# Projection stage of a window attention and ConvNeXt kernel: stores in halves on SyncE, first image quantized earlier

## The reference

```python
# layer 0: attention in windows of 7 x 7, every linear layer fake-quantized to int8
xw = x.reshape(B, C, r1, WS, r2, WS).transpose(0, 2, 4, 3, 5, 1).reshape(B * r1 * r2, n, C)
qkv = quant_linear(xw, Wqkv, bqkv)
...
out = jnp.einsum('bhmn,bhnc->bhmc', attn, v)
out = quant_linear(out, Wout, bout)          # fq(out) @ fq(Wout).T + bout: the stage that is changed
out = out.reshape(B, r1, r2, WS, WS, C).transpose(0, 5, 1, 3, 2, 4).reshape(B, C, H, W)
# layer 1: depthwise 7 x 7 convolution, layer norm, MLP with gelu and response norm, residual
y = jax.lax.conv_general_dilated(x, dw_w, (1, 1), [(3, 3), (3, 3)], feature_group_count=C, ...)
...
return residual + y
```

## Time and profile before

| | us |
|---|---|
| median of 3 runs | 5082.19 (5073.92 to 5095.0) |
| profiled execution | 5095.38 |
| its span | 5093.7 |
| projection stage, first operation to the next stage's first load | 2479.5 to 3005.1 |
| busy in the whole span: PE, DVE, ACT, POOL | 4027.8, 3922.3, 3246.1, 1504.5 |
| mean granted clock of TensorE, share of full speed | 0.90 |
| ScalarE waiting for `rd` and `yd` stores in the stage | 79.6 and 52.7 |

### The profile page before, as it was taken

One profiled execution on the slowest core, in us unless ns is written; L12 is line 12 of the kernel. 1 busy time (PEld: TensorE's weight loads), 2 busy tenths in 40 slices (PEclk: granted clock), 3 DMA queues, 4 the chain that ended last, 5 costly groups with the idle time before them and its releaser, 6 DMA issues. The chain is left out here.

```text
span 5093.7 us, 116728 instructions
## 1 busy us (share of the span) xinstructions
PE 4027.8 (79%) x40394; PEld 2551.1 (50%) x40394; DVE 3922.3 (77%) x7112; ACT 3246.1 (64%) x5602; POOL 1504.5 (30%) x1844
## 2 busy tenths in 40 slices
PE   1687777676688988888456669996689999999999
PEld 1233554454577776777444434443345455554544
DVE  7797999999999999999645520001799999999985
ACT  0675777775698988989355644443556666666663
POOL 0201111111666666666422200001232222222210
PEclk9997777876799999999777779998799999999999
DMA  7773666665333333333277778886122222222212
GB/s 316 203 204 107 160 160 166 159 163 143 79 96 94 91 94 91 94 91 94 74 256 254 279 243 290 278 278 200 63 66 90 87 90 76 76 90 87 90 55 68
DMA packets 227952, 725.18 MB, mean 142 GB/s; under 512 B 30346, under 2 KB 128138, under 8 KB 206794
## 3 DMA queue, kind: packets, MB, share of 16 engines
q1 hardware_dynamic: 203402, 589.58, 39.6%
q0 software_dynamic: 24128, 130.26, 7.1%
HBM read 428.25 MB, written 291.50 MB: 141 GB/s over the span
## 5 line engine op out<-in xcount | busy, mean ns | idle before, releaser
L852 POOL TENSOR_TENSOR exp_lo<-exp,exp_hi 128x294 f16<-128x294 f32 x1024 | 773.1, 782 | 374.8 <-ACT exp_hi L923 374.8
L1613 PE MATMUL out_psum<-gelu_hi,w_parts 128*128 128x448 f16 x2016 | 605.0, 355 | 58.9 <-DVE w_parts L1789 31.5
L1649 ACT ACTIVATE gelu_pair<-h_psum,b_rows,w_unscale 128x448 f32<-128x448 f32 x448 | 324.5, 728 | 412.5 <-PE h_psum L1565 224.7
L1685 DVE BATCH_NORM_STATS2 ln_stats<-z_img 128x6 f32<-128x192 f32 x448 | 126.0, 344 | 566.7 <-DMA z_img<-zd 565.9
L1349 PE MATMUL conv_psum<-c_in,toeplitz 128*128 128x448 f16 (+1 forms) x2304 | 470.4, 366 | 68.9 <-DMA dwb<-in_L_conv_dw_b_dram 68.9
L948 DVE SCALAR_TENSOR_TENSOR logit_int<-attn_int,scalars,bias_products 128x588 f16<-128x588 int8 x512 | 488.2, 954 | 38.6 <-ACT attn_int L929 27.0
L1565 PE MATMUL h_psum<-ln_parts_T,w_hi 128*128 128x448 f16 x2016 | 494.3, 354 | 18.1 <-DVE w_in L1748 16.2
L929 ACT ACTIVATE attn_int<-p_psum,scalars 128x588 int8<-128x588 f32 x512 | 389.4, 761 | 174.7 <-PE p_psum L455 163.7
L1613 PE MATMUL out_psum<-gelu_lo,w_parts 128*128 128x448 f16 x1344 | 475.5, 354 | 0.0
L610 PE MATMUL range_psum<-q_diag,k_diag 128*128 128x196 bf16 x1536 | 275.2, 316 | 227.8 <-DVE p_min L692 225.0
L894 PE MATMUL o_psum<-a_v,exp_hi 128*128 128x34 f16 x6144 | 382.8, 179 | 78.4 <-DVE a_o L975 66.3
(11 more groups left out here) (313 smaller groups left out, 9901.8 us busy)
## 6 DMA issues: line engine op xcount, KB each, us to landing
k_diag<-kd SPq DMA_DIRECT2D x128, 384.0 KB, 5.0
toeplitz<-gd SPq DMA_DIRECT2D x48, 1024.0 KB, 17.2
yd<-y_out POOLq DMA_DIRECT2D x16, 2880.0 KB, 28.1
c_in<-yd SPq DMA_DIRECT2D x24, 1920.0 KB, 9.4
zd<-c_out POOLq DMA_DIRECT2D x24, 1792.0 KB, 13.8
z_img<-zd SPq DMA_DIRECT2D x16, 2688.0 KB, 9.4
x_chunk<-in_x_dram SPq DMA_DIRECT2D x12, 3136.0 KB, 10.4
x_img<-in_x_dram SPq DMA_DIRECT2D x16, 2352.0 KB, 15.9
```

The costliest lines, as they stand in the source:

```text
L852: last = nc.gpsimd.tensor_tensor(el[r][:, :, 2 * a, 0:N], src[:, :, a], eh[r][:, :, 2 * a, 0:N], ALU.subtract)
L1613: last = nc.tensor.matmul(po[:, t, 0:TCH], w, hx[:, f, cols], start=f == 0 and x == 0, stop=f == NF - 1 and x == len(steps) - 1)
L1649: nc.scalar.activation(h[y // 2 % 3][:, y % 2], ph[:, y % 3, 0:TCH], ACT.Gelu, scale=k1[:], bias=b1[:, f:f + 1]).then_inc(hd, 1)
```

## The change

Three things change, all in `phase_project`.

- *Stores.* y is computed in two halves of its channels. `NY` becomes 16, eight steps (`NH`) to a half, four row pairs of 96 channels to a step; the last step of a half has one row pair. The residual is stored in two parts, its first four blocks of 448 pixels (`RTOP`) and the other three. SyncE starts these four stores of an image, each with its own semaphore, and ScalarE waits per half.
- *SyncE's order.* Six units are loaded ahead, then per image: load, first halves of y and r, load, second halves.
- *Start.* GpSimd quantizes units 0 and 1 right after clearing `o_in`, and units 2 and 3 right after the all-reduce. VectorE places four of the first image's eight bands before it waits for the all-reduce.

Moved unchanged and not shown: the bodies of `quantize` and `place`.

```diff
...
-        sty = [s.sem(f"y_stored{k}") for k in range(2)]
-        strr = [s.sem(f"r_stored{k}") for k in range(2)]
+        sty = [[s.sem(f"y_stored{k}_{h}") for h in range(2)] for k in range(2)]
+        strr = [[s.sem(f"r_stored{k}_{p}") for p in ("top", "rest")] for k in range(2)]
...
-        NY = (QP + 1) // 2
+        NQ = 4
+        NH = -(-QP // NQ)
+        NY = 2 * NH
+        CH = C // 2
+        RTOP = 4
...
-            def image(i, first):
-                for k in range(2):
-                    for hf in range(2):
-                        u = 4 * i + 2 * k + hf
-                        if not (first and k == 0):
-                            sp.wait_ge(oqd, u - 1)
-                        for h in range(2):
-                            sp.dma_start(oi[hf][64 * h:64 * h + N], s.od[bass.ds(u, 1)].rearrange("u h n j w f -> (u h) n j w f")[h]).then_inc(ld[hf], 16)
-            peeled(sp, IMG // 2, image)
+            def load(u, hf, first):
+                if not first:
+                    sp.wait_ge(oqd, u - 1)
+                for h in range(2):
+                    sp.dma_start(oi[hf][64 * h:64 * h + N], s.od[bass.ds(u, 1)].rearrange("u h n j w f -> (u h) n j w f")[h]).then_inc(ld[hf], 16)
+
+            def store_y(m, k, h):
+                half = slice(h * NCB // 2, (h + 1) * NCB // 2)
+                sp.dma_start(s.yd[half, :, bass.ds(m, 1)].rearrange("b p i c x q -> p (b i) (c x q)"),
+                             y[k][:, h * CH:(h + 1) * CH].rearrange("p (b c) x q -> p b (c x q)", c=CB)).then_inc(sty[k][h], 16)
+
+            def store_r(m, k, part, lo, hi):
+                dst = s.rd[bass.ds(m, 1)].rearrange("i (t p) n -> (i p) t n", t=2)
+                sp.dma_start(dst[:, :, lo:hi], r[k][:, :, lo:hi]).then_inc(strr[k][part], 16)
+
+            def image(i, loads):
+                for k in range(2):
+                    m = 2 * i + k
+                    if loads(k):
+                        load(2 * m + 6, 0, False)
+                    sp.wait_ge(ye, NY * m + NH)
+                    store_y(m, k, 0)
+                    sp.wait_ge(re, 2 * NTC * m + 2 * RTOP)
+                    store_r(m, k, 0, 0, RTOP * TCH)
+                    if loads(k):
+                        load(2 * m + 7, 1, False)
+                    sp.wait_ge(ye, NY * (m + 1))
+                    store_y(m, k, 1)
+                    sp.wait_ge(re, 2 * NTC * (m + 1))
+                    store_r(m, k, 1, RTOP * TCH, TOK)
+
+            for u in range(6):
+                load(u, u % 2, u < 2)
+            with sp.Fori(0, IMG // 2 - 2) as i:
+                image(i, lambda k: True)
+            image(IMG // 2 - 2, lambda k: k == 0)
+            image(IMG // 2 - 1, lambda k: False)
+            for k in range(2):
+                for part in range(2):
+                    sp.wait_ge(sty[k][part], 16 * IMG // 2)
+                    sp.wait_ge(strr[k][part], 16 * IMG // 2)
...
             for k in range(2):
                 link(nc.gpsimd.memset(oi[k][:], 0.0))
...
+            for u in range(2):
+                quantize(u, u, True)
+            pool.wait_ge(oqd, 2)
             pool.wait_ge(otz, 6)
             for k in range(2):
                 link(nc.gpsimd.memset(ot[k][0][CK:CK + NPART, 1:HW + 1, PITCH - HW:PITCH], 1.0))
             pool.wait_ge(ch, LMAX)
             nc.gpsimd.partition_all_reduce(ma[:], mp[:], P, RMAX).then_inc(ar, 1)
+            pool.wait_ge(ar, 1)
+            for u in range(2, 4):
+                quantize(u, u % 2, False)
             pool.wait_ge(ch, LCH)
             for x in range(2):
                 for t in range(2):
                     nc.gpsimd.dma_start(s.gd[x, t * CK:(t + 1) * CK, :], lines[x][:, t, :]).then_inc(lst, 16)
...
-                    pool.wait_ge(ye, NY * (m + 1))
-                    pool.wait_ge(re, 2 * NTC * (m + 1))
-                    pool.dma_start(s.yd[:, :, bass.ds(m, 1)].rearrange("b p i c x q -> p (b i) (c x q)"),
-                                   y[k][:].rearrange("p (b c) x q -> p b (c x q)", c=CB)).then_inc(sty[k], 16)
-                    pool.dma_start(s.rd[bass.ds(m, 1)].rearrange("i (t p) n -> (i p) t n", t=2), r[k][:]).then_inc(strr[k], 16)
-
-            for u in range(4):
-                quantize(u, u % 2, u < 2)
             images(pool, image)
-            for k in range(2):
-                pool.wait_ge(sty[k], 16 * IMG // 2)
-                pool.wait_ge(strr[k], 16 * IMG // 2)
             pool.wait_ge(lst, 64)

...
                     for x in range(NY):
                         if not (first and k == 0 and x < 2):
                             pe.wait_ge(ye, NY * m + x - 1)
-                        for qq in range(2 * x, min(2 * x + 2, QP)):
+                        h, q0 = x // NH, x % NH * NQ
+                        for qq in range(q0, min(q0 + NQ, QP)):
                             for t in range(2):
                                 rows = ot[k][t][:, ROWS - 2 * qq - 2:ROWS - 2 * qq, :].rearrange("p r x -> p (r x)")
-                                last = nc.tensor.matmul(py[:, (x + k * NY) % 2, qq % 2 * C:(qq % 2 + 1) * C], rows, s.woT[t][:],
+                                last = nc.tensor.matmul(py[:, x % 2, (qq - q0) * CH:(qq - q0 + 1) * CH], rows, s.woT[t][:, h * CH:(h + 1) * CH],
                                                         start=t == 0, stop=t == 1)
                         last.then_inc(ym, 1)
                         if x < 2 * NTC:
...
                     for x in range(NY):
                         act.wait_ge(ym, NY * m + x + 1)
-                        if not first and x == 0:
-                            act.wait_ge(sty[k], 16 * i)
-                        nq = min(2, QP - 2 * x)
-                        nc.scalar.activation(y[k][:, :, 0, 2 * x:2 * x + nq],
-                                             py[:, (x + k * NY) % 2, 0:nq * C].rearrange("p (q f) -> p f q", q=nq),
+                        h, q0 = x // NH, x % NH * NQ
+                        if not first and x % NH == 0:
+                            act.wait_ge(sty[k][h], 16 * i)
+                        nq = min(NQ, QP - q0)
+                        nc.scalar.activation(y[k][:, h * CH:(h + 1) * CH, 0, q0:q0 + nq],
+                                             py[:, x % 2, 0:nq * CH].rearrange("p (q f) -> p f q", q=nq),
                                              ACT.Copy, scale=ysc[:]).then_inc(yh, 1)
-                        if x == 2 * NTC:
-                            break
+                        if x >= 2 * NTC:
+                            continue
                         act.wait_ge(rm, 2 * NTC * m + x + 1)
-                        if not first and x == 0:
-                            act.wait_ge(strr[k], 16 * i)
+                        if not first and x in (0, 2 * RTOP):
+                            act.wait_ge(strr[k][x // (2 * RTOP)], 16 * i)
                         mt = x % 2
                         nc.scalar.activation(r[k][:, mt, x // 2 * TCH:(x // 2 + 1) * TCH], pr[0:CK, x % 2, 0:TCH], ACT.Identity,
                                              scale=s.syc[:, mt:mt + 1], bias=c2[:, mt:mt + 1]).then_inc(re, 1)
...
             link(v.tensor_reduce(mp[0:CK, 1:2], line[:], AX.XY, ALU.max, apply_absolute_value=True))
             assert link.count[0] == LMAX, link.count[0]
+            dve.wait_ge(ones, 5)
+            for b in range(NWIN // 2):
+                place(0, 0, b, True)
             dve.wait_ge(ar, 1)
...
             assert link.count[0] == LCH, link.count[0]
-            dve.wait_ge(ones, 5)
-
...
-            for b in range(NWIN):
+
+            for b in range(NWIN // 2, NWIN):
                 place(0, 0, b, True)
...
-                        nq = min(2, QP - 2 * x)
-                        hi, lo = (y[k][:, :, h, 2 * x:2 * x + nq] for h in range(2))
-                        v.scalar_tensor_tensor(lo, py[:, (x + k * NY) % 2, 0:nq * C].rearrange("p (q f) -> p f q", q=nq),
+                        h, q0 = x // NH, x % NH * NQ
+                        nq = min(NQ, QP - q0)
+                        hi, lo = (y[k][:, h * CH:(h + 1) * CH, part, q0:q0 + nq] for part in range(2))
+                        v.scalar_tensor_tensor(lo, py[:, x % 2, 0:nq * CH].rearrange("p (q f) -> p f q", q=nq),
                                                ysc[:], hi, ALU.mult, ALU.subtract).then_inc(ye, 1)
```

More of the change, by code:

```diff
@@ L1085, in _ @@
                 link(nc.gpsimd.memset(oi[k][:], 0.0))
-            pool.wait_ge(otz, 6)
-            for k in range(2):
-                link(nc.gpsimd.memset(ot[k][0][CK:CK + NPART, 1:HW + 1, PITCH - HW:PITCH], 1.0))
-            pool.wait_ge(ch, LMAX)
-            nc.gpsimd.partition_all_reduce(ma[:], mp[:], P, RMAX).then_inc(ar, 1)
-            pool.wait_ge(ch, LCH)
-            for x in range(2):
-                for t in range(2):
-                    nc.gpsimd.dma_start(s.gd[x, t * CK:(t + 1) * CK, :], lines[x][:, t, :]).then_inc(lst, 16)
             def quantize(u, hf, first):
@@ L1111, in image @@
```

(46 more changed lines are left out.)

## The result

The changed kernel takes 5119.95 us, the median of 18 runs (5093.05 to 5136.96), against 5087.39 of the kernel before: a ratio of 1.0064, 95% interval 1.0051 to 1.0078. The forecast was 5039, faster than before, with a range of 4988 to 5090. The measured time is 81 us above it, on the other side of no change and out of the range.

A forecast was written before the change was run, and what follows sets the result against it. The prediction took seven of 16 DMA engines, carrying every o_in load plus their part of the stores, as the projection stage's bound. Gains of 25 + 8 + 10 = 43 us off 5082.2 gave 5039, range 4988 to 5090.

The forecast's parts named there:

- 1 and 2, start and end: Projection stage: earlier quantizes land unit 6 sooner, gaining 25 us; half stores close idle gaps at the end, gaining 8.
- The seven have no idle time in steady state: Projection stage: o_in loads use seven of 16 DMA engines, which also carry stores and stay full, 29.5 to 31.9 us an image.
- 3, the halves: Middle of the stage: same bytes on the same engines, halves only shift waits, worth 0 while the seven are full.
- 4, SyncE's order: SyncE's queue: stores and loads standing behind each other's waits come 1 to 3 us late at most, covered.
- 5, the stores' rate: Stores issued by SyncE: 0.6 us an image faster, 10 us gained; best case 29 gained, worst 72 lost.
- SyncE's stores are slower: Rival, stores issued by SyncE: at the worst rate, 216 GB/s for the residual, 5121 us; chance 0.11.
- 6 and 7, TensorE, ScalarE, VectorE: Projection stage: y's narrower products add 0 to 5.4 us an image, evacuations under 1, all hidden, worth 0.
- a first quantize before 2500: Sign of being right, stage start: GpSimd's first quantize begins before 2500 us, against 2521.42 in the kernel before.
- TensorE's waits shorter: Sign of being right, projection stage: TensorE's waits are shorter but twice as many.
- a share of 0.73 to 0.75: Sign of being right, middle of the stage: DMA share alternates between 0.44 and 1.0, with 0.73 to 0.75 on the mean.
- 29 us between equal stores: Sign of being right, middle of the stage: an image takes 29 us, measured between equal stores.

The follow-up runs named there:

- e2: The changed kernel with the four half stores of an image issued by GpSimd, SyncE only loading: 5066.6 us.
- e5: The changed kernel with the residual's halves issued by GpSimd and y's halves left on SyncE: 5059.3 us.
- e3: The kernel before with the new start alone, stores as before: 5068.0 us.
- e4: The kernel before with each 49-row load of o_in cut into one of 48 rows and one of one row: 5070.1 us.
- e7: The changed kernel with the loads of units 6 to 31 issued by ScalarE, all stores still on SyncE: 5116.5 us.
- e6: The changed kernel with y's halves issued by GpSimd and the residual's halves left on SyncE: 5060.0 us.
- e13: The changed kernel, all stores on SyncE, with 98-row loads and y laid out in 128 long runs a half: 4987.2 us.
- e8: e3 with each unit loaded in one DMA of 98 rows to 98 neighbouring partitions instead of two of 49: 5014.1 us.
- e11: e5 with each unit loaded in one DMA of 98 rows instead of two of 49: 4981.3 us.
- e9: The changed kernel with each unit loaded in one DMA of 98 rows instead of two of 49, all stores on SyncE: 5025.9 us.

## Why the prediction was wrong

*1 and 2, start and end* (25 + 8 = 33). Near in sum, in part by luck: e2, which has both, is 34 us shorter in the stage than the kernel before and 21 by the medians, e5 28; but 10 of e2's 34 lie between its images 4 and 12, where these two items expect nothing. e3 has the start alone, 24 us of the stage (by the interval of the medians 4 to 34 us). But the way there was not the one told. In the changed kernel's GpSimd timeline the 7 us came on both sides of the all-reduce:

```profile
2508.48 0.37 POOL L1146 PARTITION_ALL_REDUCE y_all_max<-y_part_max  x1 [7.55 <-issue]
2515.94 0.18 POOL L1128 TENSOR_TENSOR tick<-tick 1x1 f32<-1x1 f32 x1 [7.09 <-issue]
...
2545.94 0.18 POOL L1128 TENSOR_TENSOR tick<-tick 1x1 f32<-1x1 f32 x1 [5.50 <-PE oT_psum L1180]
```

Quantize of unit 6 comes 76.9 us after the stage's start, before 88.4: 11.5 us earlier, not 25; the first y store is issued 14.6 us earlier in e3 and the last 24.4. Where the other 10 us came from was not settled. Of the end no separate figure is safe: e2 against e3 gives 10 us of the stage and 1.5 of the medians. In the changed kernel it was lost, since its last halves queue for SyncE as those of the middle do:

```profile
2998.25 6.18 SPq L1087 DMA_DIRECT2D rd<-r_out  x1
3004.47 3.48 SPq L1082 DMA_DIRECT2D yd<-y_out  x1
3007.99 8.69 SPq L1087 DMA_DIRECT2D rd<-r_out  x1
```

The last value of y is there at 2992.4 (2991.12 + 1.25 on VectorE), and its store is issued at 3004.47.

*The bound.* "The seven have no idle time in steady state" is true of their share, and I took share for work. With the new start alone the 98 rows gain 54 us, so the rate of the loads was in the bound, not the count of the engines that carry them. e4's middle has engines at 0.94 that move 268 GB/s, what they moved at 0.73:

```profile
2700.00:2800.00 100.00, 63.27 (x524) 47.38 (x522) 50.32 (x106) 59.45 (x102) 25.56 (x22) 0.79 0.94 268
```

*3, the halves* (0). Right as far as the medians tell: e2 against e3 is 1.5 us. Their profiled executions differ by 1.8 us an image, so a small gain is not excluded.

*4, SyncE's order* (0). **This step failed.** It counted who waits in SyncE's queue ("1 to 3 us late at most, covered") and gave the issue itself no time, without a reason; the loads there take 0.3 us each. The same queue was to take 3072 runs of y an image. In the changed kernel the two issues behind them hold SyncE 20 us, the loads behind the residual's stores 8 and y's own issues 3, and nothing is left of the image. Item 5 has the misreading that hid this: "y in one run of 11.5 KB a partition" is how a half lies on chip; on its way to DRAM it is the `128x12x480` of the queue listing, 12 runs of 960 bytes a partition.

The kernel before has no store of short runs on SyncE, but its trace shows the hold in the next stage. There SyncE issues a load of 4 KB (`dwb`) behind two of 1024 runs of 1024 bytes each:

```profile
3042.92 3.36 SPq L1320 DMA_DIRECT2D toeplitz<-gd  x2
3046.46 8.78 SPq L1321 DMA_DIRECT2D dwb<-in_L_conv_dw_b_dram  x1
```

The 24 issues of `dwb` hold SyncE 9.1 us in the median. This does not give a price of a run, which is not the same everywhere (see e7). It does show that an issue behind many short runs is not free. Some 9 us for each half (an estimate by these rows) belonged into the sum as a bound.

*5, the stores' rate* (-10, bounds -29 and +72). The term is +53 by the medians, +67 in the stage, inside its bounds, nearer to its worst than to the value taken. `xq`, its nearest row, was near in bytes and rows and far in runs (one of 12544 bytes a partition). The rival "SyncE's stores are slower" gave 5121 and the time is 5120, but by the wrong mechanism: its 216 GB/s for the residual are refuted by e6, where the residual on SyncE costs nothing. A range that ends half way into a rival of that size is too narrow when its price is unknown.

The Trainium skill (DMA: Bandwidth & Descriptors, section "Issuing engines are not separate DMA queues") says that issuing on several engines saves only the sequencer's time, "usually small relative to the DMA itself". e13 agrees with the first part; in the changed kernel that time is 10.0 us for a store that lands in 22, and with the stores on GpSimd (e2) the loss is gone.

*6 and 7, TensorE, ScalarE, VectorE* (0). Right. Eight products of 96 columns take 0.53 us at full clock (four of 192: 0.50):

```profile
2641.34 0.53 PE L1197 MATMUL y_psum<-woutT,oT 99*128 99x96 bf16 x8 [1.57 <-DVE oT L1254]
```

Of the signs named ahead, a first quantize before 2500 (2485), "TensorE's waits shorter" (its weight loads wait for ScalarE's evacuation of r 27 times, 3.2 us at most; before 9 times, up to 12.7) and a share of 0.73 to 0.75 came true in a kernel that got slower: they did not tell the cases apart. The 29 us between equal stores did; it was 33.1.

## What to carry to other kernels

Before a transfer is moved to another engine's queue, count its contiguous runs, not its bytes or rows, on the DRAM side of the transfer, look in the trace for an issue on that queue that stands behind as many, and add up what one turn of the loop then asks of the issuing engine. An engine that never waits on its semaphores may be the bound; a run with part of its work elsewhere (e2, e5) tells. Read the DMA share only beside GB/s: 160 and 183 GB/s stood beside 0.99 and 0.44. And look at which partitions a load writes: two loads of 49 partitions, one after the other, ran at 183 GB/s, one load of 98 at 289.

## What the runs showed that was not expected

- An issue on SyncE behind a DMA of many short runs is held: 0.8, 5.5, 10.0 and 22 us behind 128, 768, 1536 and 3072 runs; with the loads in another queue (e7) 14.1 behind 1536. GpSimd issues the same y half in 1.09 us (e2) and the whole in 1.49.
- Loads of 49 rows to 49 partitions: 183 GB/s at a DMA share of 0.44. Of 48 + 1 rows: 160 at 0.99. Of 98 rows: 289 at 0.90. The 98 rows were worth 54 us in e8 against e3, 78 in e11 against e5, 94 in e9 against the changed kernel.
- GpSimd stands still 7.55 us ahead of a `partition_all_reduce` and 7.09 us behind it, where an ordinary operation is its neighbour and the profile shows nothing else that it waits for.
